# One lane of four looked up whole, three lanes gathered over all partitions, in the edge layer of a graph network

## The chip, the cores and the metric

The kernel runs on one core of one Trainium2 chip. The metric is device time in microseconds (us) for one whole execution, lower is better. All views below come from one profiled execution, whose trace holds start, length and semaphore events of every instruction.

## The reference, cut to what matters

```python
h = maximum(layernorm(x), 0)                                  # 12500 nodes x 32
e = concatenate([h[src], h[dst], edge_attr], axis=-1)         # 400000 edges x 96, dst is sorted
v = relu(e @ W1 + b1) @ W2 + b2                               # 96 -> 64 -> 32
out = x + maximum(segment_max(v, dst), x)                     # per node, the maximum over its edges
```

For every edge, layer one needs the row of `h` of its source node. The sources are random, so these 400000 rows of 32 floats have to be fetched one by one. Everything is f32.

## The kernel before, in words

**Tiling.** The 400000 edges are cut into 4 lanes of 100000 (A = 4), one for each quarter of the 128 partitions (32 features each). A *pair* is two blocks (g = 0 and 1) of 512 edges in each lane, so 4096 edges. There are 96 full pairs (0 to 95), a short one (96) and four mini pairs (97 to 100). In what follows a pair has its number in the program, j.

**Two ways to fetch a source row.** Of each block of 512 edges in each lane, 384 are *gathered* (GATHERED): GpSimd (POOL) issues indirect DMAs of 128 rows each, 12 a block, 24 a pair, one for each of 12 columns of indices (`gather_burst`, the calls at L665), into the ring `src_in` of 7 slots (AHEAD). The gathers of a pair may start once its ring slot has been turned (`src_turned`), and each burst of 2 waits for a count of looked-up tiles (`gather_pair`, L682). VectorE transposes a slot into `src_t` (`turn_src`, L1278). The other 128 edges of each block and lane (4 x 128 = 512 a block) are *looked up*: TensorE multiplies the table of all nodes, held in SBUF, with one-hot columns (`look_up`, L925, matmuls at L939; 98 of them a pair, 128x128 by 512 columns, in four chunks c = 0 to 3). The one-hot columns come from ScalarE (L848, L853) and VectorE (L1251); VectorE then picks from the looked-up rows (`mask_rows`, L1265, at L1269 and L1276) and leaves `picked_rows`, in which all 128 partitions hold a share of a row, so that the matmul with `w_src` (the weights stacked four times) sums over all 128.

**Layer one** of a pair (`layer_one`, L945): for each lane a and block g, W1's three parts are added up in the bank `ps_hid[a]`, half g: edge features (L954, 32 rows x 64 columns of weights, 512 columns of edges), destination (L958, the same), gathered sources (L964, 384 columns), looked-up sources (L969, all 128 rows, 128 columns each, 8 matmuls). The matmuls of 32 rows work side by side in 8 parts of the array (4 lanes x 2 blocks), those of 128 rows in 2 (the blocks). The profile counts each f32 matmul as two. After each lane `hid_summed` lets ScalarE apply the ReLU (`relu_pair`, L834). TensorE's order in pair j is: layer one of j, chunk 0 of the look-up of j+2, layer two of j (L1007), chunks 1 to 3 of the look-up of j+2. Pairs 97 to 100 have no gathered edges (`layer_one_mini`, L981, L983, L987: there all matmuls write half 0, one after the other).

**Loads.** SyncE (SP) issues nearly all loads and stores in one written-out order (`feed`, L591): edges, first rows, picks for j+3, then, for j % 7 == 4 (IX_AT), it waits for the gathers of pair j+2 (the last ring slot) and loads the next 7 pairs' indices (`load_indices`, L450, 4 DMAs at L453), then the mask of j+2 (L477) and the store of j. At k = 1 to 11 of the first turn one more large DMA each fills `run_max` (L622). At the start SP and ScalarE load the first indices (L494, L768, two DMAs each), wait for them, and only then issue the loads of `dst` (L496, L770).

**The end.** When enough pairs are stored, POOL gathers each node's maximum (L749, 98 indirect DMAs, the last 7 only after all 101 pairs are stored), VectorE adds bias and x in 14 steps (L1475 to L1479), and the result is stored.

## Time and profile before

| what | us |
|---|---|
| median of 3 runs | 3179.54 (3175.47 to 3183.26) |
| the profiled execution, its own time | 3179.01 |
| its span in the trace | 3177.2 |
| PE busy (matmuls) | 3042.7 (96%) |
| POOL busy | 2387.1 (75%) |
| DVE (VectorE) busy | 2212.8 (70%) |
| ACT (ScalarE) busy | 2182.5 (69%) |
| mean granted share of TensorE's clock | 0.983 |

How to read it: the busy share of POOL counts only the instructions; the pause after each of them, in which its queue fetches and prepares the next, is not counted. A busy PE is one on which some matmul is under way, and several can be at once. What sets the time has to be read from waits and from the pace of each engine.

### The profile page before, as it was taken

The numbers are of one execution on the slowest core, as the hardware profiler recorded it, in microseconds if no ns is written. First come the engines' busy times: TensorE is split into PE (matmuls) and PEld (weight loads), VectorE is DVE, ScalarE is ACT, GpSimd is POOL, SyncE is SP. The second block draws the span as 40 slices with busy tenths as digits, with TensorE's granted clock in tenths as the row PEclk, the third lists the DMA queues.
The fourth block names the chain that finished last, engine by engine and source line by source line (L and its number), as shares of the span: only waits on it lengthen the run. The fifth ranks groups of instructions, "written<-read, shape, count | busy, mean of one in ns | idle before, by whom it ended". The sixth has DMA issues, their size and how long they took to land.

```text
span 3177.2 us, 59073 instructions
## 1 busy us (share of the span) xinstructions
PE 3042.7 (96%) x19778; PEld 2247.9 (71%) x19778; DVE 2212.8 (70%) x2474; ACT 2182.5 (69%) x2555; POOL 2387.1 (75%) x2523
## 2 busy tenths in 40 slices
PE   6999899998999999999999999999898897999996
PEld 4776677776777777777777777777676675777674
DVE  5321677776777777777777777777675775777666
ACT  3334677776777777777777777777676675777674
POOL 7777677777777777777777777777777777777776
PEclk9999999999999999999999999999999998999998
DMA  8951355444343333334443334333342443333323
GB/s 255 357 201 27 75 138 136 130 117 116 96 104 103 99 96 97 99 102 104 103 104 98 101 101 103 98 96 95 97 103 51 127 102 80 96 103 100 78 65 65
DMA packets 226637, 350.67 MB, mean 110 GB/s; under 512 B 97248, under 2 KB 147708, under 8 KB 226346
## 3 DMA queue, kind: packets, MB, share of 16 engines
q1 hardware_dynamic: 142691, 303.74, 32.6%
q0 software_dynamic: 80448, 41.33, 8.2%
q10 hardware_dynamic: 3332, 4.01, 0.5%
q14 instruction: 139, 1.14, 0.1%
q8 instruction: 27, 0.44, 0.1%
HBM read 240.36 MB, written 119.78 MB: 113 GB/s over the span
## 4 chain that ended last, share of the span: by engine, by line
PE 87%; POOL 5%; DVE 2%; issue 2%; DMA 2%; SPq 1%; ACTq 0%; ACT 0%; POOLq 0%; DVEq 0%
PE ps_rows L939 66%; PE ps_layers L913 4%; PE ps_layers L919 4%; PE ps_layers L954 3%; PE ps_layers L969 3%; PE ps_layers L1007 3%; PE ps_layers L958 3%; POOL src_in L749 3%; POOL src_in L665 2%; PE ps_layers L964 2%; SPq L463 1%; DVE onehot L1251 1%; DMA src_in<-h_dram,src_ix 1%; DMA picks<-picks_dram 0%; DMA dst_i<-in_dst_dram 0%
## 5 line engine op out<-in xcount | busy, mean ns | idle before, releaser
L665 POOL DMA_INDIRECT src_in<-h_dram,src_ix x2269 | 2144.9, 945 | 700.9 <-issue 629.5
L939 PE MATMUL ps_rows<-onehot,table 128*128 128x512 f32 x9898 | 2317.8, 393 | 54.0 <-DVE onehot L1251 54.0
L939 PEld LDWEIGHTS ps_rows<-onehot,table 128*128 128x128 f32 x9898 | 1851.1, 189 | 536.1 <-issue 109.5
L853 ACT ACTIVATE onehot<-distance 128x1024 fp32r<-128x1024 bf16 x909 | 905.4, 1049 | 686.7 <-PE ps_rows L939 681.5
L848 ACT ACTIVATE distance<-picks,below_column 128x1024 bf16<-128x1024 int16 x909 | 983.7, 1136 | 67.8 <-DMA picks<-picks_dram 67.8
L1251 DVE SCALAR_TENSOR_TENSOR onehot<-picks,column,ps_layers 128x1024 fp32r<-128x1024 int16 x404 | 507.6, 1277 | 315.7 <-PE ps_rows L939 302.3
L1301 DVE STREAM_TRANSPOSE ps_layers<-rows_in 128x512 f32<-128x512 f32 x202 | 133.2, 705 | 262.9 <-ACT hid L839 194.4
L1306 DVE TENSOR_TENSOR_SCAN dst_t<-mask_in,dst_t,ps_layers 128x512 f32<-128x512 bf16 (+1 forms) x198 | 250.6, 1266 | 7.3
L839 ACT ACTIVATE hid<-ps_layers,b_col 128x512 f32<-128x512 f32 (+1 forms) x404 | 238.1, 665 | 25.4 <-PE ps_layers L969 13.8
L1319 DVE TENSOR_TENSOR_SCAN max_t<-mask_in,max_t,ps_layers 128x512 f32<-128x512 bf16 x196 | 248.8, 1269 | 4.1 <-PE ps_layers L1007 0.2
L1269 DVE SCALAR_TENSOR_TENSOR picked_rows<-picks,fold,ps_rows 128x512 f32<-128x512 int16 x202 | 141.8, 743 | 113.8 <-PE ps_rows L939 113.8
L1324 DVE STREAM_TRANSPOSE rows_in<-max_t 128x512 f32<-128x512 f32 x202 | 216.8, 1112 | 3.5
L1292 DVE STREAM_TRANSPOSE ea_t<-rows_in 128x512 f32<-128x512 f32 x202 | 204.7, 1086 | 0.0
L825 ACT ACTIVATE signs<-ps_layers,below_node 128x640 bf16<-128x640 f32 x98 | 77.7, 793 | 170.1 <-PE ps_layers L919 162.4
L913 PE MATMUL ps_layers<-ea_t,rows_in 125*128 125x320 bf16 x980 | 153.5, 303 | 25.4 <-DVE rows_in L1076 20.5
L1286 DVE STREAM_TRANSPOSE src_t<-src_in 128x384 f32<-128x384 f32 x193 | 154.4, 871 | 25.4 <-DMA src_in<-h_dram,src_ix 25.4
L919 PE MATMUL ps_layers<-dst_t,rows_in 125*128 125x320 bf16 x980 | 151.2, 302 | 0.0
L1276 DVE COPY_PREDICATED picked_rows<-of_side,ps_rows 128x512 f32<-128x512 int16 x202 | 136.8, 732 | 18.9 <-DVE picked_rows L1269 18.6
L913 PEld LDWEIGHTS ps_layers<-ea_t,rows_in 125*128 125x128 bf16 x980 | 96.2, 99 | 66.2 <-issue 21.1
L954 PE MATMUL ps_layers<-ea_t,w_edge 32*64 32x512 f32 x1552 | 110.7, 627 | 26.4 <-DVE onehot L1251 26.4
L1260 DVE SCALAR_TENSOR_TENSOR of_side<-picks,fold,ps_layers 128x1024 int16<-128x1024 int16 x101 | 128.7, 1274 | 0.0
L1174 DVE TENSOR_SCALAR tmp<-above 128x7 f32<-128x7 f32 x14 | 2.6, 183 | 177.1 <-ACT block L827 177.1
(145 smaller groups left out, 1146.5 us busy)
## 6 DMA issues: line engine op xcount, KB each, us to landing
picks<-picks_dram SPq DMA_DIRECT2D x101, 512.0 KB
first_rows<-hid SPq DMA_DIRECT2D x100, 500.0 KB
rows_in<-in_edge_attr_dram SPq DMA_DIRECT2D x384, 128.0 KB
rows_in<-first_rows SPq DMA_DIRECT2D x384, 128.0 KB
run_max<-rows_in SPq DMA_DIRECT2D x384, 128.0 KB
src_in<-h_dram,src_ix POOLq DMA_INDIRECT x2269
mask_in<-mask_dram SPq DMA_DIRECT2D x384, 64.0 KB
run_max<-in_edge_attr_dram SPq DMA_DIRECT2D x10, 1024.0 KB
```

The source lines that it names most:

```text
L665: pool.indirect_dma_start(out=src_in[:, slot, g, r, :], out_offset=None, in_=rows[:, :], in_offset=bass.IndirectOffsetOnAxis(ap=src_ix[:, ...
L839: nc.scalar.activation(hid[rows, a, columns], ps_hid[a][rows, columns], ACT.Relu, bias=b1_col[rows, 0:1]).then_inc(hid_made, 1)
L848: nc.scalar.activation(distance[:, k, :], picks[:, slot, 0, :, :].rearrange("p g w -> p (g w)"), ACT.Abs, bias=below_column[:, i:i + 1]).t ...
L853: nc.scalar.activation(onehot[:, RING_AT[c] + BY_DVE[c] + k, :, :].rearrange("p g w -> p (g w)"), distance[:, k, :], ACT.Relu, bias=1.0, s ...
L913: nc.tensor.matmul(ps_hid[j % 2 * 2 + half][:, 0:HALF + half], step[:, hb % 2, t, k * P:(k + 1) * P], rise_hi[:, t, half * HALF:(half + 1) ...
L919: mm = nc.tensor.matmul(ps_hid[j % 2 * 2 + half][:, 0:HALF], step[:, hb % 2, t, k * P:(k + 1) * P], rise_lo[:, t, half * HALF:(half + 1) * ...
L939: mm = nc.tensor.matmul(ps_rows[g][side][:, 0:WIDE], table[:, i * SIDES + side, part, :], onehot[:, RING_AT[c] + t, g, :], start=(i + part ...
L954: nc.tensor.matmul(ps_hid[a][g * HID:(g + 1) * HID, :], w_edge[chunk(a), :], ea_t[chunk(a), slot, g, :], start=True, stop=False)
L1251: compared = V.scalar_tensor_tensor(out=onehot[:, RING_AT[c] + t, :, :].rearrange("p g w -> p (g w)"), in0=picks[:, slot, 0, :, :].rearran ...
L1306: V.tensor_tensor_scan(dst_t[:, slot, g, 0:n], mask_in[:, slot, g, 0:n], ps_first[:, g, 0:n], state, ALU.min, ALU.max).then_inc(dst_filled ...
L1319: V.tensor_tensor_scan(max_t[:, g, 0:n], mask_in[:, slot, g, 0:n], v[g][:, 0:n], state, ALU.min, ALU.max).then_inc(max_scanned, 2 // len(c ...
L1324: V.transpose(max_out[:, slot, h, :, :], of_half(max_t[:, :, :], h)).then_inc(max_turned, 1)
```

## The change

The lanes are no longer all treated alike. In a full pair, lanes 0 to 2 have all 512 edges of a block gathered: the first 384 into their own quarter of the partitions as before, the other 128 into the fourth quarter (columns a*4 to a*4+3 of its 12 index columns). Lane 3 (WHOLE) has all 512 looked up. The number of indirect DMAs (24 a pair), of looked-up columns and of one-hot work stays. In layer one the gathered part becomes 6 matmuls of 384 columns (32 rows), each counting up a new semaphore `own_summed`; then 2 matmuls of 128 rows by 512 columns for lane 3; then, after a wait of TensorE on `own_summed`, 6 matmuls of 32 rows by 128 columns that read the rest of lanes 0 to 2 from the fourth quarter of `src_t`, 4 neighbouring columns out of every 12. Lane 3 is now the first for which `hid_summed` counts up, and ScalarE takes the lanes in the order 3, 0, 1, 2. The index loads become 6 DMAs in place of 4 (three of 48-byte pieces, three of 16-byte pieces); the load of the looked-up indices becomes one DMA in place of four. The short and the mini pairs stay as they were.

```diff
--- before.py
+++ after.py
@@ -370,7 +373,9 @@
...
         ea_view, first_view, max_view = (row_view(t) for t in (edge_attr, first_rows, run_max))
-        ix_view = [bass.AP(src.tensor, STARTS[a], [[GATHERS, LANES], [BLK, 2 * SHORT_AT + 1], [1, GATHERS]]).bitcast(U32) for a in range(A)]
+        ix_view = [bass.AP(src.tensor, STARTS[a], [[GATHERS, LANES], [BLK, 2 * SHORT_AT], [1, GATHERS]]).bitcast(U32) for a in range(WHOLE)]
+        rest_ix_view = [bass.AP(src.tensor, STARTS[a] + GATHERED, [[PICKS, LANES], [BLK, 2 * SHORT_AT], [1, PICKS]]).bitcast(U32) for a in range(WHOLE)]
+        half_ix_view = [bass.AP(src.tensor, STARTS[a] + tail_start(SHORT_AT), [[GATHERS, LANES], [1, GATHERS]]).bitcast(U32) for a in range(A)]
         short_ix_view = [bass.AP(src.tensor, STARTS[a] + tail_start(SHORT_AT) + BLK, [[1, LANES], [1, 1]]).bitcast(U32) for a in range(A)]
...
@@ -404,6 +409,14 @@
...
         OUT_STORES = A * len(OUT_BATCHES) + 1
+        def own_ix(a, half):
+            return src_ix[chunk(a), half, :, :, :].rearrange("l s g r -> l (s g) r")
+        def rest_ix(a, half):
+            return src_ix[chunk(WHOLE), half, :, :, a * PICKS:(a + 1) * PICKS].rearrange("l s g r -> l (s g) r")
         def by_rows(t, r):
...
@@ -448,11 +461,13 @@
             def load_indices(j, half, loaded, last=False):
-                blocks = 2 * AHEAD - 3 if last else 2 * AHEAD
-                for a in range(A):
-                    sp.dma_start(src_ix[chunk(a), half, :, :, :].rearrange("l s g r -> l (s g) r")[:, 0:blocks],
-                                 ix_view[a][:, bass.ds(j * 2, blocks)]).then_inc(loaded, D)
-                    if last:
+                blocks = 2 * AHEAD - 4 if last else 2 * AHEAD
+                for a in range(WHOLE):
+                    sp.dma_start(own_ix(a, half)[:, 0:blocks], ix_view[a][:, bass.ds(j * 2, blocks)]).then_inc(loaded, D)
+                    sp.dma_start(rest_ix(a, half)[:, 0:blocks], rest_ix_view[a][:, bass.ds(j * 2, blocks)]).then_inc(loaded, D)
+                if last:
+                    for a in range(A):
+                        sp.dma_start(src_ix[chunk(a), half, AHEAD - 2, 0, :], half_ix_view[a]).then_inc(loaded, D)
                         sp.dma_start(src_ix[chunk(a), half, AHEAD - 2, 1, 0:1], short_ix_view[a], allow_slow_non_contiguous=True).then_inc(loaded, D)
...
@@ -490,19 +505,20 @@
...
                              bass.AP(x.tensor, 0, [[HB * F, LANES - FULL_Q - 1], [1, HB * F]])).then_inc(x_loaded, D)
-            for a in range(A // 2):
-                sp.dma_start(src_ix[chunk(a), 0, 0, :, :], ix_view[a][:, 0:2]).then_inc(first_ix_loaded, D)
-            sp.wait_ge(first_ix_loaded, A * D)
+            for a in range(WHOLE):
+                sp.dma_start(own_ix(a, 0)[:, 0:2], ix_view[a][:, 0:2]).then_inc(first_ix_loaded, D)
+            sp.wait_ge(first_ix_loaded, 2 * WHOLE * D)
             sp.dma_start(dst_i[1:1 + PIECE, 0:SEARCH], dst_before[0:PIECE]).then_inc(dst_loaded, D)
             sp.dma_start(dst_i[1 + PIECE:BP, 0:SEARCH], dst_before[PIECE:BP - 1]).then_inc(dst_loaded, D)
-            for a in range(A):
-                sp.dma_start(src_ix[chunk(a), 0, 1:AHEAD, :, :].rearrange("l s g r -> l (s g) r"), ix_view[a][:, 2:2 * AHEAD]).then_inc(early_ix_loaded, D)
+            for a in range(WHOLE):
+                sp.dma_start(own_ix(a, 0)[:, 2:2 * AHEAD], ix_view[a][:, 2:2 * AHEAD]).then_inc(early_ix_loaded, D)
+                sp.dma_start(rest_ix(a, 0)[:, 2:2 * AHEAD], rest_ix_view[a][:, 2:2 * AHEAD]).then_inc(early_ix_loaded, D)
             sp.wait_ge(dst_loaded, 4 * D)
...
             clear(0, 3)
-            for a in range(A):
-                sp.dma_start(pick_i[0:SHORT_AT, :, a, :], bass.AP(src.tensor, STARTS[a] + GATHERED, [[2 * BLK, SHORT_AT], [BLK, 2], [1, PICKED]])).then_inc(picks_read, D)
+            sp.dma_start(pick_i[0:SHORT_AT, :, :, :].rearrange("j g a e -> j (g a e)"),
+                         bass.AP(src.tensor, STARTS[WHOLE], [[2 * BLK, SHORT_AT], [1, 2 * BLK]])).then_inc(picks_read, D)
             for g, at in enumerate((GATHERED, BLK + SHORT_GATHERED)):
...
@@ -764,9 +780,9 @@
...
         def _(act):
-            for a in range(A // 2, A):
-                act.dma_start(src_ix[chunk(a), 0, 0, :, :], ix_view[a][:, 0:2]).then_inc(first_ix_loaded, D)
-            act.wait_ge(first_ix_loaded, A * D)
+            for a in range(WHOLE):
+                act.dma_start(rest_ix(a, 0)[:, 0:2], rest_ix_view[a][:, 0:2]).then_inc(first_ix_loaded, D)
+            act.wait_ge(first_ix_loaded, 2 * WHOLE * D)
             act.dma_start(dst_i[0:PIECE, SEARCH:SEARCH + BE], dst_rows[0:PIECE]).then_inc(dst_loaded, D)
...
@@ -831,11 +847,12 @@
...
             act.wait_ge(weights_loaded, D * (3 * A + 5))
-            def relu_pair(j, mini=False):
+            def relu_pair(j, mini=False, short=False):
                 wait(act, v_summed, j)
                 rows, columns = (slice(0, HID), slice(0, MINI)) if mini else (slice(0, P), slice(0, BLK))
-                for a in range(A):
-                    act.wait_ge(hid_summed, j * A + (a + 1))
+                order = list(range(A)) if mini or short else [WHOLE, *range(WHOLE)]
+                for n, a in enumerate(order):
+                    act.wait_ge(hid_summed, j * A + (n + 1))
                     nc.scalar.activation(hid[rows, a, columns], ps_hid[a][rows, columns], ACT.Relu, bias=b1_col[rows, 0:1]).then_inc(hid_made, 1)
...
@@ -958,7 +975,28 @@
...
                 pe.wait_ge(src_turned, j * 2 + 2)
-                gathered = [GATHERED, SHORT_GATHERED if short else GATHERED]
+                if short:
+                    short_sources(j, slot)
+                    return
+                for g in range(2):
+                    for a in range(WHOLE):
+                        nc.tensor.matmul(ps_hid[a][g * HID:(g + 1) * HID, 0:GATHERED], w_src[chunk(a), :], src_t[chunk(a), g, :],
+                                         start=False, stop=False).then_inc(own_summed, 1)
+                pe.wait_ge(rows_masked, j * MASKS + MASKS)
+                for g in range(2):
+                    mm = nc.tensor.matmul(ps_hid[WHOLE][g * HID:(g + 1) * HID, :], w_src[:, :], picked_rows[:, slot, g, :], start=False, stop=True)
+                mm.then_inc(hid_summed, 1)
+                pe.wait_ge(own_summed, j * (2 * WHOLE) + 2 * WHOLE)
+                for a in range(WHOLE):
+                    for g in range(2):
+                        rest = src_t[chunk(WHOLE), g, :].rearrange("p (l r) -> p l r", r=GATHERS)[:, :, a * PICKS:(a + 1) * PICKS]
+                        mm = nc.tensor.matmul(ps_hid[a][g * HID:(g + 1) * HID, GATHERED:BLK].rearrange("p (l r) -> p l r", r=PICKS),
+                                              w_src[chunk(WHOLE), :], rest, start=False, stop=True)
+                    mm.then_inc(hid_summed, 1)
+            def short_sources(j, slot):
+                gathered = [GATHERED, SHORT_GATHERED]
                 for g in range(2):
```

## Rows read from the trace of the kernel before

**Rows 1.** The page: busy time, the chain that ended last, the ReLUs' group.
```profile
PE 3042.7 (96%) x19778; PEld 2247.9 (71%) x19778; DVE 2212.8 (70%) x2474; ACT 2182.5 (69%) x2555; POOL 2387.1 (75%) x2523
PE 87%; POOL 5%; DVE 2%; issue 2%; DMA 2%; SPq 1%; ACTq 0%; ACT 0%; POOLq 0%; DVEq 0%
...
L839 ACT ACTIVATE hid<-ps_layers,b_col 128x512 f32<-128x512 f32 (+1 forms) x404 | 238.1, 665 | 25.4 <-PE ps_layers L969 13.8
```

**Rows 2.** Timeline, PE: layer one's first matmuls (start, length) of pairs 14, 68, 69, 76, 83, 95, 96.
```profile
761.04 0.69 PE L954 MATMUL ps_layers<-ea_t,w_edge 32*64 32x512 f32 x8
2233.79 0.68 PE L954 MATMUL ps_layers<-ea_t,w_edge 32*64 32x512 f32 x8
2272.67 0.68 PE L954 MATMUL ps_layers<-ea_t,w_edge 32*64 32x512 f32 x8
2483.21 0.69 PE L954 MATMUL ps_layers<-ea_t,w_edge 32*64 32x512 f32 x8
2694.87 0.69 PE L954 MATMUL ps_layers<-ea_t,w_edge 32*64 32x512 f32 x8
3034.41 0.69 PE L954 MATMUL ps_layers<-ea_t,w_edge 32*64 32x512 f32 x8 [1.42 <-DVE onehot L1251]
3061.69 0.69 PE L954 MATMUL ps_layers<-ea_t,w_edge 32*64 32x512 f32 x8
```

**Rows 3.** POOL: busy time and count in one stretch; all gathers of L665 by form.
```profile
500.00:2900.00 2400.00, 1814.20 (x1923) 0.99 0.40 101
L665 POOL DMA_INDIRECT src_in<-h_dram,src_ix x2269: 938/944/1618, 72.7 to 3043.3; - x190
L665 POOL DMA_INDIRECT src_in<-in_x_dram,src_ix x48: 940/944/2412, 3.3 to 66.4; - x48
```

**Rows 4.** Waits from 290 us on: of PE; of DVE from 470 to 3045 us; of SP's queue.
```profile
PE ps_rows L939 <- DVE onehot L1251: 54.0, 5, 17.8
PE ps_layers L954 <- DVE onehot L1251: 26.4, 7, 9.0
...
DVE ps_layers L1301 <- DMA mask_in<-mask_dram: 68.4, 3, 26.0
DVE src_t L1286 <- DMA src_in<-h_dram,src_ix: 25.4, 6, 5.7
...
SPq L608 <- DMA src_in<-h_dram,src_ix: 160.3, 9, 32.9
```

**Rows 5.** Timeline, PE, of layer one in an undisturbed pair (j = 42) and after it.
```profile
1524.69 1.11 PE L954 MATMUL ps_layers<-ea_t,w_edge 32*64 32x512 f32 x16
1525.60 1.06 PE L958 MATMUL ps_layers<-dst_t,w_dst 32*64 32x512 f32 x16
1526.46 0.85 PE L964 MATMUL ps_layers<-src_t,w_src 32*64 32x384 f32 x16
1527.24 1.09 PE L969 MATMUL ps_layers<-picked_rows,w_src 128*64 128x128 f32 x16
1528.26 3.92 PE L939 MATMUL ps_rows<-onehot,table 128*128 128x512 f32 x16
```

**Rows 6.** Timeline, PE, of the looked-up matmuls of a mini pair (one column half only).
```profile
3089.96 1.96 PE L987 MATMUL ps_layers<-picked_rows,w_src 128*64 128x128 f32 x16
3091.85 0.50 PE L939 MATMUL ps_rows<-onehot,table 128*128 128x512 f32 x1
```

**Rows 7.** Timeline of the start (0 to 16 us), and of SP around its one long block.
```profile
0.76 0.87 SPq L494 DMA_DIRECT2D src_ix<-in_src_dram  x2
3.08 0.37 ACTq L770 DMA_DIRECT2D dst_i<-in_dst_dram  x1
...
671.64 1.90 SPq L453 DMA_DIRECT2D src_ix<-in_src_dram  x4
...
688.16 23.69 SPq L463 DMA_DIRECT2D rows_in<-in_edge_attr_dram  x4
...
731.88 2.02 PE L954 MATMUL ps_layers<-ea_t,w_edge 32*64 32x512 f32 x16 [8.99 <-DVE onehot L1251]
```

**Rows 8.** Timeline of the end: last stores, start of VectorE's last steps, POOL, last step.
```profile
3148.62 5.42 SPq L586 DMA_DIRECT2D run_max<-rows_in  x8
3152.49 0.19 DVE L1466 COPY ps_rows<-b_row 128x32 f32<-128x32 f32 x1
3155.91 0.26 SPq L642 DMA_DIRECT2D carry<-run_max  x1
3158.19 1.16 POOL L749 DMA_INDIRECT src_in<-run_max,gather_ix  x1 [0.30 <-issue]
3168.35 0.39 DVE L1475 TENSOR_TENSOR src_in<-src_in,ps_rows 128x224 f32<-128x224 f32 x1 [0.65 <-DMA src_in<-run_max,gather_ix]
```

More of the change, by code:

```diff
@@ L37 @@
 PICKED = PICKS * LANES
+WHOLE = A - 1
+assert A * PICKED == BLK and WHOLE * PICKS == GATHERS
 MINIS = 4
@@ L350, in build @@
         hid_summed, hid_made, v_summed, layers_begun = sem("hid_summed"), sem("hid_made"), sem("v_summed"), sem("layers_begun")
+        own_summed = sem("own_summed")
         max_scanned, max_turned, ends_set = sem("max_scanned"), sem("max_turned"), sem("ends_set")
@@ L692, in gather_turn @@
             def gather_turn(turn, half, loads, last=False):
-                pool.wait_ge(ix_loaded[half], loads * (A * D))
+                pool.wait_ge(ix_loaded[half], loads * (2 * WHOLE * D) + last * (2 * A * D))
                 pool.sem_inc(gathers_begun, 1)
@@ L698, in gather_turn @@
                     gather_pair(half, slot, turn * (AHEAD * TILES) + (slot + 2 - AHEAD) * TILES - SLACK, last and slot == AHEAD - 2)
-            pool.wait_ge(first_ix_loaded, A * D)
+            pool.wait_ge(first_ix_loaded, 2 * WHOLE * D)
             gather_early(0)
-            pool.wait_ge(early_ix_loaded, A * D)
+            pool.wait_ge(early_ix_loaded, 2 * WHOLE * D)
             for j in range(1, RAW_PAIRS):
@@ L735, in _ @@
                 gather_turn(i * 2 + 2, 0, i + 1)
-            gather_turn(TURNS - 1, 1, TURNS // 2 + 1, last=True)
+            gather_turn(TURNS - 1, 1, TURNS // 2, last=True)
             pool.wait_ge(low_row_written, D)
@@ L854, in one_hot, with pair @@
                                          distance[:, k, :], ACT.Relu, bias=1.0, scale=-1.0).then_inc(act_onehot_made, 1)
-            def pair(j, slot, turn, next_again=True, after_next=True, mini=False):
-                relu_pair(j, mini)
+            def pair(j, slot, turn, next_again=True, after_next=True, mini=False, short=False):
+                relu_pair(j, mini, short)
                 if next_again:
@@ L881, in _ @@
             for j in range(SHORT_AT, PAIRS):
-                pair(j, j % 2, j // 2, next_again=j + 2 < PAIRS, after_next=j + 3 < PAIRS, mini=j > SHORT_AT)
+                pair(j, j % 2, j // 2, next_again=j + 2 < PAIRS, after_next=j + 3 < PAIRS, mini=j > SHORT_AT, short=j == SHORT_AT)
             act.wait_ge(onehot_made, PAIRS * DVE_ALL)
@@ L1126, in _ @@
             V.memset(table_f[:, UNITS - 1, :], 0.0).then_inc(table_padded, 1)
-            dve.wait_ge(picks_read, (A + 3) * D)
+            dve.wait_ge(picks_read, 4 * D)
             V.tensor_copy(pick_16[:, :], pick_i[:, :, :, :].rearrange("j g a e -> j (g a e)")).then_inc(pick_step, 1)
```

## The prediction

> **What bounds the kernel now.** I read the page first. TensorE is busy 96% of the span and fills 87% of the chain that ended last, POOL 5% [rows 1]. That reads as "TensorE is the bound", and it is half the truth, so I took the pace of each engine next. TensorE: from pair 14 to pair 68 are 54 pairs in 2233.79 - 761.04 = 1472.75 us, 27.27 us a pair [rows 2]. POOL: 1923 gathers in 2400 us, 1.248 us each although one is busy for only 0.944 [rows 3], and with 24 gathers 29.95 us a pair. POOL is the slower of the two by 2.68 us a pair; its 75% is a full engine. It is hidden at first because the gathers have a head start of up to seven ring slots.
>
> How far ahead POOL is can be worked out. Its last gather is number 2269 + 48 = 2317, starts at 3043.3 [rows 3], and pair j's last gather is number 24(j + 1), so it ends at 3043.3 - (2317 - 24(j + 1)) x 1.248 + 0.9. For pair 68 that is 2219.3, and TensorE begins its layer one at 2233.79 [rows 2]: a lead of 14.5 us. For pair 95 it is 3028.0, against 3034.41: 6.4 us, which is what landing, transposes and the one-hot columns behind them take. So the lead is used up towards the end and TensorE waits. Its waits are always booked on VectorE's one-hot (L1251), 54.0 and 26.4 us [rows 4]; but VectorE itself was held by mask loads (68.4 us in 3 waits) and by gathers (25.4 us in 6). The mask loads are late because SP, before every seventh pair's index load, sits until the gathers of two pairs ahead have landed (L608, up to 32.9 us), with that mask queued behind. Once the lead falls under about 24 us, this blocks: pair 69 starts at 2272.67 where 2261.06 was due, with a lead of 23.4; the blocks before pairs 76 and 83 leave 24 to 26.3 [rows 2]. Together: 81 pairs from pair 14 at 27.27 would bring pair 95 to 2970.2; it starts at 3034.41. **64.2 us of TensorE's time are slack behind the gathers.** That is the number on which the change turns.
>
> At the end three ends nearly meet: the last store and with it the signal for POOL's last 7 gathers falls at about 3155.9, POOL gets to them at 3158.19, and VectorE's last steps, begun at 3152.49, wait 0.65 us for the last gather [rows 8]. If TensorE is late by X, the end is late by X - 0.65.
>
> **The change, term by term.** First layer one of a full pair [rows 5].
>
> (1) *Gathered part*, 6 matmuls instead of 8: no gain. The 8 run side by side; edges and destination take 0.86 to 0.91 us for two turns (high and low part) of 512 columns, so 0.43 a turn, and 384 columns 0.32. With the fourth quarter idle a turn is as long.
>
> (2) *Looked-up part.* Now 8 turns of 128 columns (each with both halves side by side), 1.02 us from first start to the next look-up. In a mini pair the 16 have only one half, one after another: 1.89 us [rows 6]. The difference, 0.87 us for 8 turns, gives 0.109 us a turn, and 1.02 - 8 x 0.109 = 0.15 us for coming into and out of such a phase. After the change: 2 turns of 512 columns, 0.86 in place of 0.87: -0.01.
>
> (3) *The rest*, 6 matmuls of 128 columns in the fourth quarter. They share it, so both halves run side by side but the three lanes and the two parts one after another: 6 turns x 0.109 = 0.65 us, plus 0.15 for one more phase. Nothing hides it: the matmuls before and after use all rows. +0.80. The reads jump by 12 columns after every 4, which no matmul here does. From below such a turn costs 0.109, as the contiguous 128 columns of [rows 5, 6]; from above I bound it by a matmul over the whole 384 columns that the read steps across, 0.32 us a turn, +1.28 more a pair. I take the lower end, as the nearest row in columns moved. By the Trainium skill (page "SBUF — State Buffer", the note on SBUF cachelines) the SBUF is read in 16-byte lines and four f32 may be strided over for free, which here would be the lower end too, as each run of four begins on such a line; no row here shows it.
>
> (4) *The new wait* on `own_summed`: behind it on TensorE are the rest, the look-up, everything. But it asks for matmuls that ended before the looked-up phase (0.86 us) began: 0.
>
> (5) *Order of the ReLUs*: ScalarE gets lane 3 first and lanes 0 to 2 within the next 0.65 us; its four ReLUs (0.665 us each [rows 1], 2.7 in all) are needed only by layer two, behind 32 look-up matmuls (16 take 3.9 us [rows 5]). 0. With that cover gone, the later start would cost its 0.65 us.
>
> So TensorE needs **0.79 us more a pair**, for 96 pairs.
>
> (6) *Start.* SP and ScalarE issue three index DMAs each instead of two before the loads of dst; two take 0.87 us [rows 7], so +0.43 before everything. The picks' load, one DMA for four, lies behind cover: no row has anything waiting for it.
>
> (7) *Index loads in the loop*: 4 DMAs take 1.90 us, 6 take 2.85, every seventh pair. The index DMAs stand ahead of the mask load and the store; the mask of pair j+2 is needed only about a pair later, so 0.95 us is covered except in the three blocks, where it would be added each time; these vanish, see below. 0. POOL's gathers stay 24 a pair of 128 rows: 0.
>
> (8) *SP's long issue* at 688.16 (23.69 us) behind the last large fill stops TensorE once for 8.99 us [rows 7]. It stays, but is hung on pair 11's store, and TensorE is one pair's 0.79 later when it gets there: -0.8.
>
> **The sum.** Before pair 95's layer one lie 95 x 0.79 = 75.0; less 0.8, plus 0.43, less the slack of 64.2: +10.4. Pair 95 itself +0.79, the last slack -0.65: **+10.6 us**. Against the profiled execution's 3179.01 (0.5 under the median of 3179.54): 3189.6; I say 3190 for the median.
>
> Check that the slack is really free: the blocks go, as with +0.79 a pair the lead at pair 83 would be -26 (761.04 + 69 x 27.27 = 2642.9 against 2668.6) + 66 - 1 = 39 us, above 26. At pair 95 it is 16, above 6.4: TensorE is then the bound, by 9 us. POOL's own end moves by +0.43 and, since early gathers wait for a transposed ring slot, by about one pair's 0.79.
>
> **The rivals.** All turn on the extra time d of a pair. TensorE's end moves by 96 d - 65.2; the gathers' end by about +1.4; they meet at d = 0.69, and 0.3% (9.5 us, about what a measurement can tell from no change) is reached at d = 0.78.
>
> *A. Forecast*, d 0.72 to 0.87: +4 to +18, centre +10.6. Chance 0.50.
>
> *B. Not slower: the gathers still set the end.* Place: the last pairs and POOL's tail; price +1.4 us, so about 3181; it decides for d under 0.69, for instance if the switch out of the looked-up phase is partly covered (its 0.15 off gives d = 0.64), or if SP's one long block no longer reaches TensorE (-9 us, from 10.6 to 1.6). For it: the 64.2 us are real and the margin small. Against: the 0.65 us of turns alone are nearly 0.69, and a third phase has never been free in these rows. 0.22.
>
> *C. The six counts of `own_summed` hold up the switch.* They fall within one turn, right before the looked-up phase, where now none falls. Price between 0, as the phase start already waits a little for VectorE, and one more phase change of 0.15 a pair: 96 x 0.15 = +14, so +25, 3204. For: no row has six counts together; against: counts of single matmuls cost nothing visible in [rows 5]. 0.17. The Trainium skill (page "TensorE: Matmul & The Clock Gate", section "The cost: per-tile semaphore tail") says that such increments are written one after another, 26.3 ns each; by an estimate from that page six would add 0.16 us a pair, and the sum would be about +26.
>
> *D. The jumping reads are slow*: up to 1.28 a pair more, +134 us; even a quarter of it +41. 0.08.
>
> *E. Faster* by over 9.5 us: would need POOL's pace to change, and nothing touches it. 0.03.
>
> **How the numbers follow.** Prediction 3190, A's centre. Slower by over 0.3%: a bit over half of A (0.28), C, D: 0.53. Within 0.3%: rest of A, B: 0.44. Faster 0.03. The range 3180 to 3210 leaves out D, E and C's upper part. A alone: 3184 to 3198.
>
> **What would show it.** Right: pairs 28.06 us apart; L939 following three phases instead of two; the rest 0.80 us; the three late blocks gone, PE's waits down from 80 to under 35 us; PE not waiting before pair 95, a lead there of about 16 us; POOL waiting before its last 7 gathers. B: pairs under 27.96 apart and pair 95 still about 6 us behind its gathers. C: the gap between gathered and looked-up phase longer than the 0.78 us of now. D: the rest's turns longer than 0.109. Wrong altogether if POOL's 1.248 us moves.

## The result, and the profile after

The changed kernel takes 3187.88 us (median of 8 runs, 3185.26 to 3189.22) against 3179.04 (8 runs, 3175.47 to 3183.26) for the kernel before: a ratio of 1.0027, interval 1.0016 to 1.0037, or 8.8 us slower. That interval straddles the 0.3% below which I had said a measurement could not tell it from no change, but it does not reach 1: the change makes the kernel a little slower. One execution of all, of the run with the rest in its own quarter below, took 4330.07 us at a granted clock of 0.667, and is left out of its median. The profiled execution took 3185.75 us with a span of 3183.9; that of before 3179.01 with 3177.2, so the two traces differ by 6.7 us. Everything below is read from these two traces unless it says otherwise.

From the page of the changed kernel: the busy row, the shares of the chain that ended last, and the groups of the look-up's and layer one's first matmuls (columns: busy us, mean ns | idle us before them, and what ended it).

```profile
PE 3104.8 (98%) x19394; PEld 2237.0 (70%) x19394; DVE 2210.6 (69%) x2474; ACT 2181.9 (69%) x2555; POOL 2392.4 (75%) x2523
PE 95%; DVE 2%; DMA 1%; SPq 1%; issue 0%; ACTq 0%; ACT 0%; DVEq 0%
...
L956 PE MATMUL ps_rows<-onehot,table 128*128 128x512 f32 x9898 | 2308.5, 392 | 10.1 <-DVE onehot L1289 10.1
...
L971 PE MATMUL ps_layers<-ea_t,w_edge 32*64 32x512 f32 x1552 | 109.8, 622 | 15.9 <-DVE onehot L1289 15.9
```

Beside [rows 1] and [rows 4]: TensorE is busy for 62.1 us more with 384 matmuls fewer, its waits on the one-hot columns went from 80.4 to 26.0 us, and POOL, 5% of the chain before, is in it no longer. (The profile writes each f32 matmul down twice, so these are 384 records.) TensorE paid for the change mainly with time in which it had been waiting. The 54.4 us of waits that went are not all of the 64.2 us of slack, though. The other 10 were lost in the kernel before when TensorE came back from a wait at half its clock. In its timeline the stop before pair 69 reads

```profile
2261.18 11.56 PE L939 MATMUL ps_rows<-onehot,table 128*128 128x512 f32 x42 [9.56 <-DVE onehot L1251]
```

9.56 us of waiting, and pair 69 came 11.61 us late. The granted clock was 0.50 (1.2 GHz) from 2255 to 2264 us, in the wait and for 2.8 us of work behind it, 0.78 up to 2266, and 1.00 (2.4 GHz) from there to 2273. Over the whole span the granted clock is 0.991 in the changed kernel, for 0.983.

The price of a pair comes first, from the timeline of TensorE: pairs 14, 68, 95 and 96 (start, length), which answer to [rows 2].

```profile
769.40 0.69 PE L971 MATMUL ps_layers<-ea_t,w_edge 32*64 32x512 f32 x8
...
2283.92 0.68 PE L971 MATMUL ps_layers<-ea_t,w_edge 32*64 32x512 f32 x8
...
3041.18 0.69 PE L971 MATMUL ps_layers<-ea_t,w_edge 32*64 32x512 f32 x8
...
3069.22 0.69 PE L971 MATMUL ps_layers<-ea_t,w_edge 32*64 32x512 f32 x8
```

The 54 pairs take 1514.52 us, 28.047 each; before it was 27.273. So d = 0.774 us, and it stays so to the end: pair 95 begins 28.04 before pair 96, where [rows 2] had lost 64.2 us on the way. (d is the extra time of a pair, as in the prediction.) Where the 0.774 lie is in TensorE's timeline of one undisturbed pair, which answers to [rows 5].

```profile
1526.66 1.11 PE L971 MATMUL ps_layers<-ea_t,w_edge 32*64 32x512 f32 x16
1527.57 1.06 PE L975 MATMUL ps_layers<-dst_t,w_dst 32*64 32x512 f32 x16
1528.43 0.84 PE L983 MATMUL ps_layers<-src_t,w_src 32*64 32x384 f32 x12
1529.20 1.08 PE L987 MATMUL ps_layers<-picked_rows,w_src 128*64 128x512 f32 x4
1530.21 0.87 PE L993 MATMUL ps_layers<-src_t,w_src 32*64 32x128 f32 x12
1531.01 3.24 PE L956 MATMUL ps_rows<-onehot,table 128*128 128x512 f32 x13
```

From start to start: gathered 0.77 (before 0.78), looked-up 1.01 (1.02), and the new phase, the rest, 0.80. The two old phases kept their lengths to the hundredth, though one has a quarter of its matmuls fewer and the other went from 16 to 4 records; the third came on top whole.

What stood behind the gathers before now stands in front of them. These are waits of TensorE and of SP's queue from 290 us on, and of VectorE from 470 to 3052 us (in total, times, longest), beside [rows 4].

```profile
PE ps_layers L971 <- DVE onehot L1289: 15.9, 2, 8.9
PE ps_rows L956 <- DVE onehot L1289: 10.1, 2, 5.1
...
SPq L624 <- DMA src_in<-h_dram,src_ix: 28.0, 3, 15.0
...
DVE ps_layers L1339 <- ACT hid L856: 195.1, 92, 5.4
```

SP's wait for gathers fell from 160.3 us in 9 to 28.0 in 3, and VectorE's 68.4 us on mask loads and 25.4 on gathers have no row any more. TensorE's remaining 26.0 us are waits at the start and the one behind SP's long block. The end, beside [rows 8], from the timeline of VectorE and of POOL:

```profile
3160.04 0.17 DVE L1504 COPY ps_rows<-b_row 128x32 f32<-128x32 f32 x1
...
3164.18 0.95 POOL L765 DMA_INDIRECT src_in<-run_max,gather_ix  x1 [2.60 <-SPq L657]
```

POOL, which came to its last 7 gathers late in [rows 8], now stands there for 2.60 us waiting for SP's signal: it is ahead.

### The profile page after: what moved, and what is told of

Its sections match the earlier page's. It is cut to its first block, busy times and chain, and to the rows that moved or that the text cites. A ratio compares the mean times of both kernels' runs of the same rounds, so it can differ in the third digit from the quotient of the medians.

```text
span 3183.9 us, 58462 instructions
## 1 busy us (share of the span) xinstructions
PE 3104.8 (98%) x19394; PEld 2237.0 (70%) x19394; DVE 2210.6 (69%) x2474; ACT 2181.9 (69%) x2555; POOL 2392.4 (75%) x2523
## 4 chain that ended last, share of the span: by engine, by line
PE 95%; DVE 2%; DMA 1%; SPq 1%; issue 0%; ACTq 0%; ACT 0%; DVEq 0%
PE ps_rows L956 71%; PE ps_layers L930 4%; PE ps_layers L936 4%; PE ps_layers L971 3%; PE ps_layers L1045 3%; PE ps_layers L987 3%; PE ps_layers L975 3%; PE ps_layers L993 2%; PE ps_layers L983 2%; SPq L478 1%; DMA picks<-picks_dram 0%; DMA dst_i<-in_dst_dram 0%; DVE onehot L1289 0%; DMA x_again<-in_x_dram 0%; ACTq L833 0%
```

## The experiments

Each run was compared with the kernel before on its own chip, whose median differs between chips (3177.72, 3183.19 and 3184.25 for the runs below): ratios are to be compared, and the traces' own times more than either.

### Two gathers fewer a pair: is POOL the bound of before and not of after?

The twelfth gather of each block is not issued, so a pair has 22. The rows that it would have brought count as zero: a part of the gathered sources is left out of layer one. On the kernel before:

```diff
+ISSUED = GATHERS - 1
...
             def gather_row(half, slot, g, r, rows=h_dram):
+                if r == GATHERS - 1:
+                    return
...
-                        dve.wait_ge(src_gathered[k % AHEAD][g], turn * (2 * D * GATHERS) + (k // AHEAD + 1) * (D * GATHERS))
+                        dve.wait_ge(src_gathered[k % AHEAD][g], turn * (2 * D * ISSUED) + (k // AHEAD + 1) * (D * ISSUED))
```

> The kernel before with 22 gathers a pair instead of 24 (the twelfth index column of each block isn't fetched, its rows stay zero). My theory (the gather stream is what TensorE waits for, 64 us of slack): POOL needs 22 x 1.248 = 27.5 us a pair, about TensorE's 27.27, so the lead is never used up, the three late blocks and the waits before pairs 91 to 95 go, and the time falls by about 60 us, to 3110 to 3125. Rival (TensorE is the bound as the page's 96% suggests, and its late waits come from SP's order and not from the gathers' pace): within 5 us of before.

Measured: 3112.74 us against 3183.19, ratio 0.9776 (0.976 to 0.9792), 70.5 us faster. From this run's timeline and waits of TensorE:

```profile
760.31 0.68 PE L960 MATMUL ps_layers<-ea_t,w_edge 32*64 32x512 f32 x8
...
2969.44 0.69 PE L960 MATMUL ps_layers<-ea_t,w_edge 32*64 32x512 f32 x8
...
PE ps_layers L960 <- DVE onehot L1258: 16.7, 2, 9.7
PE ps_rows L945 <- DVE onehot L1258: 10.0, 2, 5.1
```

The 81 pairs from 14 to 95 take 2209.13 us, 27.273 each, with no late stop among them; pair 95 begins at 2969.44, where the prediction had worked out 2970.2 for a TensorE that waits for no gather. TensorE's waits are 26.7 us, those of the changed kernel. The 64.2 us are slack behind the gathers, and this run shows it from the side of POOL. The spans of the two traces differ by 65.6 us (3111.6 for 3177.2); the medians differ by more because the kernel before takes 3183.19 on this chip.

The same edit on the changed kernel, with the same rows left out:

> The changed kernel with the same 22 gathers a pair. My theory (with 28.05 us a pair TensorE alone sets the end): no more than 3 us faster than the changed kernel, so 3183 to 3189, and about 70 us (96 x 0.77, less what the gathers' start gives) slower than the same edit on the kernel before. Rival (the gathers still set part of the time after the change): 10 us or more faster than the changed kernel.

Measured: 3187.78 us, ratio 1.0014 (1.0004 to 1.0023), pairs 28.047 us apart, pair 95 at 3043.39: the changed kernel's time, with two gathers fewer. It is 75.0 us behind the run above; 96 pairs at 0.774 are 74.3. So the change costs TensorE all of its 0.774 us a pair, and the kernel as a whole shows only the few us that stand out over the slack.

### What in the third phase costs the 0.80 us

First, the rest in its own lanes' quarters: each lane's 128 last columns are taken from its own gathered rows, of which they read the first 128 a second time, and its six matmuls follow the gathered part at once. Layer one's sum of the last 128 columns of three lanes so holds other rows; the number and the size of the matmuls are the same. Two more things change with the order: TensorE no longer waits on `own_summed`, and ScalarE starts its four ReLUs, in the order 0 to 3, only behind the looked-up matmuls.

```diff
+                for g in range(2):
+                    for a in range(WHOLE):
+                        mm = nc.tensor.matmul(ps_hid[a][g * HID:(g + 1) * HID, GATHERED:BLK], w_src[chunk(a), :], src_t[chunk(a), g, 0:PICKED],
+                                              start=False, stop=True)
+                mm.then_inc(hid_summed, 1)
                 pe.wait_ge(rows_masked, j * MASKS + MASKS)
...
-                pe.wait_ge(own_summed, j * (2 * WHOLE) + 2 * WHOLE)
```

> The changed kernel, but the 6 matmuls of 128 columns for the rest of lanes 0 to 2 read (other) data from their own lanes' quarters, right behind the 384 columns and ahead of the looked-up phase: the same number of matmuls and columns, but side by side in six parts of the array and with no phase change of their own, so what is computed for these edges is wrong. My theory (the 0.77 us a pair are the six turns one after another in one quarter, 0.65, and one more phase change, 0.15): the pair's extra falls to two turns, about 0.2 us (period 27.45 to 27.55), the gathers set the end again, and the time is that of before plus 0 to 3 us, 3178 to 3183. Rival (the cost is the new order, the semaphore own_summed with its six counts, or lane 3's late sum): the pair stays above 27.9 us, 3184 or more.

Measured: 3183.51 us against 3183.19, ratio 1.0001 (0.9992 to 1.0011), pairs 27.467 us apart. The time lies 0.5 us over the range that I had expected, and close to the rival's, because the kernel before is slow on this chip; the 27.467, which the rival had over 27.9, is what decides. TensorE's timeline of a pair:

```profile
1535.31 0.84 PE L983 MATMUL ps_layers<-src_t,w_src 32*64 32x384 f32 x12
1535.96 0.42 PE L987 MATMUL ps_layers<-src_t,w_src 32*64 32x128 f32 x12
1536.30 1.08 PE L992 MATMUL ps_layers<-picked_rows,w_src 128*64 128x512 f32 x4
```

Side by side and in the gathered phase, the same six matmuls cost 0.19 us instead of 0.774. With only that on TensorE the gathers set the end again: the late stops are back (16.9 us before pair 76, 21.9 before 83), pair 95 begins 6.2 us behind its gathers, for 6.4 before, and the time is that of before.

Next, the same reads, but in a phase of their own behind the looked-up matmuls, so that only the quarter differs from the changed kernel. Again the last 128 columns of three lanes take other rows:

```diff
-                        rest = src_t[chunk(WHOLE), g, :].rearrange("p (l r) -> p l r", r=GATHERS)[:, :, a * PICKS:(a + 1) * PICKS]
+                        rest = src_t[chunk(a), g, 0:PICKED].rearrange("p (l r) -> p l r", r=PICKS)
...
-                                              w_src[chunk(WHOLE), :], rest, start=False, stop=True)
+                                              w_src[chunk(a), :], rest, start=False, stop=True)
```

> The changed kernel, order and waits untouched, but each rest matmul reads (other) data from its own lane's quarter with that quarter's weights, so that the six work side by side though still in a phase of their own behind the looked-up one. Together with the run that also moved them ahead (pair 27.47 us) it splits the 0.77 us: theory, the turns one after another in one quarter are 6 x 0.109 and shrink to 2 x 0.109 = 0.22, the phase change of 0.15 stays, so a pair is 27.27 - 0.01 + 0.22 + 0.15 = 27.63 us, and as that is below 27.96 the gathers set the end: time of before within 3 us. Rival (a phase of its own costs more, and the turns less): 27.75 us or more.

Measured: 3183.33 us against 3184.25, ratio 1.0001 (0.9991 to 1.0011), pairs 27.680 us apart. TensorE's timeline of a pair:

```profile
1544.26 1.08 PE L987 MATMUL ps_layers<-picked_rows,w_src 128*64 128x512 f32 x4
1545.27 0.46 PE L993 MATMUL ps_layers<-src_t,w_src 32*64 32x128 f32 x12
1545.66 6.68 PE L956 MATMUL ps_rows<-onehot,table 128*128 128x512 f32 x28
```

The phase takes 0.39 us from start to start instead of 0.80. The pair lies between my 27.63 and the rival's 27.75. The two runs split d: 0.37 us for turns taken one after another in one quarter (28.047 - 27.680), 0.21 for a phase of its own behind matmuls of 128 rows (27.680 - 27.467), 0.19 for the turns that there would be in any place (27.467 - 27.273). Only the first is a difference in one thing. The wait on `own_summed` and the order of the ReLUs change together with the place, so that the 0.21 is put down to the phase change because no wait of TensorE shows at that place in the traces, and not because a run changed it alone. By turns of 0.109 the first would be 4 x 0.109 = 0.44, the last 2 x 0.109 = 0.22; they came out a little cheaper, and the phase change dearer than my 0.15. The Trainium skill (page "TensorEngine Tiling (Array Packing)", section "Key Properties") says that changing the tiling mode drains TensorE; the 0.21 us is what one more such phase, with the change into it and out of it, was worth here, and the traces agree that it is not free.

Then the jumping reads, rival D. The rest reads 128 neighbouring columns of the fourth quarter, so again other rows enter the last 128 columns of three lanes:

```diff
-                        rest = src_t[chunk(WHOLE), g, :].rearrange("p (l r) -> p l r", r=GATHERS)[:, :, a * PICKS:(a + 1) * PICKS]
+                        rest = src_t[chunk(WHOLE), g, a * PICKED:(a + 1) * PICKED].rearrange("p (l r) -> p l r", r=PICKS)
```

> The changed kernel whose rest matmuls read 128 neighbouring columns of the fourth quarter instead of 4 out of every 12 (so the rows that lanes 0 to 2 get for these edges are not theirs). Theory (jumps of 12 columns after every 4 are free): pairs 28.05 us apart, time of the changed kernel within 3 us. Rival D in small (the jump costs something within the 0.80 us): the rest's phase shorter than 0.80 us.

Measured: 3187.72 us, ratio 1.0032 (1.002 to 1.0044), pairs 28.047 us apart, and in TensorE's timeline the rest again takes 0.80 us:

```profile
1532.44 0.87 PE L993 MATMUL ps_layers<-src_t,w_src 32*64 32x128 f32 x12
1533.24 3.01 PE L956 MATMUL ps_rows<-onehot,table 128*128 128x512 f32 x12
```

Runs of four f32 with steps of twelve cost nothing here. This is what the note on cachelines of the Trainium skill (page "SBUF — State Buffer") would give for runs that begin on a line of 16 bytes; no run tried shorter runs. D is out.

### The wait and its counts

Rival C said that six counts just ahead of the looked-up phase hold up the switch. One count on the last gathered matmul in their place:

```diff
-                        nc.tensor.matmul(ps_hid[a][g * HID:(g + 1) * HID, 0:GATHERED], w_src[chunk(a), :], src_t[chunk(a), g, :],
-                                         start=False, stop=False).then_inc(own_summed, 1)
+                        own = nc.tensor.matmul(ps_hid[a][g * HID:(g + 1) * HID, 0:GATHERED], w_src[chunk(a), :], src_t[chunk(a), g, :],
+                                               start=False, stop=False)
+                own.then_inc(own_summed, 1)
...
-                pe.wait_ge(own_summed, j * (2 * WHOLE) + 2 * WHOLE)
+                pe.wait_ge(own_summed, j + 1)
```

> The changed kernel with one count of own_summed, on the last of the six gathered matmuls, instead of six. In the changed kernel the looked-up phase starts 0.77 us after the gathered one, as before (0.78), so the six counts should cost nothing: pairs stay 28.05 us apart, the time that of the changed kernel (3185 to 3190). Rival C of the prediction (six counts hold up the switch): up to 0.15 us a pair less, and up to 14 us faster.

Measured: 3188.01 us, ratio 1.0032 (1.002 to 1.0045), pairs 28.047 us apart, every phase as long as in the changed kernel:

```profile
1530.38 0.84 PE L983 MATMUL ps_layers<-src_t,w_src 32*64 32x384 f32 x12
1531.16 1.08 PE L988 MATMUL ps_layers<-picked_rows,w_src 128*64 128x512 f32 x4
1532.17 0.87 PE L994 MATMUL ps_layers<-src_t,w_src 32*64 32x128 f32 x12
```

C is out. The section "The cost: per-tile semaphore tail" of the Trainium skill (page "TensorE: Matmul & The Clock Gate"), read as a cost of this place, gave an estimate of 0.16 us a pair for six counts; the runs show nothing of it, with six or with one (28.047 us a pair in both).

That left the order. With the rest directly behind the gathered part, two phases of 32 rows stand together, which I expected to save one phase change; the price would be a wait that is no longer covered by the looked-up matmuls.

```diff
                                          start=False, stop=False).then_inc(own_summed, 1)
-                pe.wait_ge(rows_masked, j * MASKS + MASKS)
...
                 pe.wait_ge(own_summed, j * (2 * WHOLE) + 2 * WHOLE)
...
                     mm.then_inc(hid_summed, 1)
+                pe.wait_ge(rows_masked, j * MASKS + MASKS)
```

> The changed kernel with the rest's 6 matmuls right behind the gathered ones, in the same 32-row phase, and the looked-up 2 matmuls last; ReLUs in the order 0, 1, 2, 3. One phase change fewer (0.15 us a pair), but now the wait on own_summed stands directly behind the matmuls that count it, so their way through the array (a 384-column matmul is booked 0.48 us where its turn takes 0.32) lies open, about 0.16 plus the count. Theory: the two about cancel, a pair is 27.95 to 28.1 us, the time within 5 us of the changed kernel. Rival 1 (only the phase change counts): 27.9 us a pair, 14 us less for TensorE, of which the gathers leave about 7: 3178 to 3183. Rival 2 (the looked-up rows' wait for VectorE was on the way, and is now covered too): a further 0.05 a pair less.

Measured: 3215.03 us against 3177.72, ratio 1.0121 (1.0105 to 1.0136), pairs 28.354 us apart: 0.31 us more than the changed kernel, where I had expected about none. TensorE's timeline of a pair and, below, the row of its waits:

```profile
1512.74 0.84 PE L983 MATMUL ps_layers<-src_t,w_src 32*64 32x384 f32 x12
1513.81 0.87 PE L989 MATMUL ps_layers<-src_t,w_src 32*64 32x128 f32 x12 [0.23 <-PE ps_layers L983]
1514.61 1.08 PE L994 MATMUL ps_layers<-picked_rows,w_src 128*64 128x512 f32 x4
1515.62 7.55 PE L956 MATMUL ps_rows<-onehot,table 128*128 128x512 f32 x32
...
PE ps_layers L989 <- PE ps_layers L983: 22.2, 96, 0.2
```

The rest starts 1.07 us after the gathered part, of which two turns of 384 columns are 0.64. That leaves 0.43 us, in the place of the 0.13 that the step to the looked-up phase took in the changed kernel (0.77 - 0.64), and so the pair is 0.30 us longer. Of the 0.43 the wait's row shows 0.23 a pair. That the other 0.20 belong to the wait as well, as the end of the last matmul and the start of the next, is my reading: no run has this order without the wait, and the nearest, the rest in its own quarter, had 0.65 us from start to start with none. The rest itself still takes 0.80 and the looked-up part 1.01. So term (4) of the prediction, the wait at 0, holds only because looked-up matmuls stand between; this run is that cover taken away.

### The start, and an attempt at POOL's one hold

The changed kernel began pair 0 2.34 us earlier than before, and the load of the looked-up indices (the picks) is the only part of the start that the change makes smaller. Four loads of 512-byte pieces again:

```diff
-            sp.dma_start(pick_i[0:SHORT_AT, :, :, :].rearrange("j g a e -> j (g a e)"),
-                         bass.AP(src.tensor, STARTS[WHOLE], [[2 * BLK, SHORT_AT], [1, 2 * BLK]])).then_inc(picks_read, D)
+            for a in range(A):
+                sp.dma_start(pick_i[0:SHORT_AT, :, a, :], bass.AP(src.tensor, STARTS[WHOLE] + a * PICKED, [[2 * BLK, SHORT_AT], [BLK, 2], [1, PICKED]])).then_inc(picks_read, D)
```

> The changed kernel with the looked-up indices loaded by four DMAs of 512-byte pieces, as before, instead of one of 4096-byte pieces. In the trace of the changed kernel the reload of the table from h_dram starts 3.2 us earlier than before (67.2 against 70.5 us) and layer one of pair 0 at 363.8 instead of 366.1, though the loads of dst start 0.5 us later. Theory (the one large DMA clears the queues sooner for the store of h): both go back, the table's reload to about 70.5, pair 0 to about 366.5, and the time is 2 to 3 us longer than the changed kernel's. Rival (scatter from run to run): no shift of more than 1 us in the median, and pair 0 starts anywhere from 363 to 367.

Measured: 3188.0 us, ratio 1.0015 (1.0005 to 1.0024); pair 0 begins at 365.03. The two kernels were then run again, with a profile each, to see how far two executions of one kernel differ:

> The changed kernel once more, for the scatter of its start and of the gathers' pace. Theory: pairs 28.05 us apart as always, the start of pair 0 anywhere from 363 to 367 us, the median within 1 us of 3188 whatever the chip. Rival: the pace of the pairs itself scatters.

> The kernel before once more, with its trace. Theory: pairs 27.27 us apart up to pair 68, then waits; pair 0 starts anywhere from 363 to 367 us (no gain of the changed kernel's start), and its median differs from chip to chip by a few us (3179 and 3183 so far) because it ends with the gathers. Rival: pair 0 again at 366 and the table's reload at 70.4 us, so that the changed kernel's earlier start is real.

Measured: 3187.25 us, ratio 1.0013 (1.0004 to 1.0023), for the changed kernel, and 3183.22, ratio 1.0 (0.999 to 1.0009), for the one before. Pair 0 began at 365.57 in the changed kernel and at 363.94 in the one before, the other way round than in the first two traces; over all thirteen traces it lies between 363.8 and 366.6 with no order by kernel. No shift of 2.34 us between the kernels is left over this scatter, and nothing speaks for the theory of the picks' load any more.

Last, an attempt to win something at POOL, whose gathers are held once at 350 us for 7.5 us. The hold seemed to be the count of look-up tiles, so the kernel before was run with gathers released 13 tiles earlier:

```diff
-SLACK = 6
+SLACK = 19
```

> The kernel before with SLACK 19 instead of 6: each burst of gathers is released 13 looked-up tiles (one pair) earlier; the ring slot's own wait for the transposes stays. Theory (the gather stream sets the end of the kernel before, and the only time it stands still is about 9 us between 300 and 480 us, held by TensorE's tile count): the standstill shrinks by up to 9 us and the time with it, 3170 to 3180 against about 3179 to 3183. Rival (the hold is the ring slot, not the tile count, or TensorE and not the gathers sets the end): no change beyond 2 us.

Measured: 3177.53 us against 3177.72, ratio 1.0001 (0.9992 to 1.001). POOL came to this gather 4.7 us earlier, and its hold is 3.5 us longer. From POOL's timeline of this run:

```profile
357.77 0.95 POOL L665 DMA_INDIRECT src_in<-h_dram,src_ix  x1 [10.98 <-PE ps_rows L939]
```

in the kernel before, the same gather stood as

```profile
358.99 0.94 POOL L665 DMA_INDIRECT src_in<-h_dram,src_ix  x1 [7.47 <-PE ps_rows L939]
```

The release waits on something that the tile count does not move, and the traces point at the ring slot. In both traces 168 gathers stand before this one, 7 slots of 24, so it is the first that needs a slot a second time. VectorE begins the two transposes of `src_t` at 356.43 us in the kernel before and at 355.23 in this run, and the gather starts 2.56 and 2.54 us behind that. The slot was not released earlier in a run of its own. No version that computes the whole and beats the kernel before was found.

## Why the prediction was right

**What it turned on held.** The hinge was stated as 96 d - 65.2 for TensorE's end, with the gathers' end taking over below d = 0.69. The first result and the seven runs made from the changed kernel with all 24 gathers give four values of d, each with the kernel before of its own chip:

```text
kernel                    d       96 d - 65.2   measured against before
rest in own quarter       0.19        -47          +0.3   gathers set the end
own quarter, last         0.41        -26          -0.9   gathers set the end
changed (first result)    0.774        +9.1        +8.8
changed, again            0.774        +9.1        +3.0
changed, four pick loads  0.774        +9.1        +4.8
changed, read straight    0.774        +9.1       +10.0
changed, one count        0.774        +9.1       +10.3
rest ahead of looked-up   1.08        +38.5       +37.3
```

Below the hinge the time doesn't move. Above it, between two kernels on one chip (one count and rest ahead), it grows by 27.0 us for 0.307 us of d, so 88 us per us for the 96 forecast. The five rows at 0.774 spread by 7 us though the five medians of the changed kernel and its variants agree within 1: it is the kernel before that differs from chip to chip. That the first result came so near to the forecast of 10.6 is in part luck, as on another chip the difference was 3.0. Rival B is out for the changed kernel: its pairs are 28.047 apart and pair 95 begins 9.7 us behind its gathers, not 6. Its place was real, though: the runs with the rest in its own quarter are in it.

**Terms (1) to (3), the price of a pair.** Predicted 0.79, measured 0.774. Gathered and looked-up part -0.01 each for the 0 and -0.01 forecast, the rest 0.80 for 0.80. The sum inside the 0.80 was less exact than it looks: the phase change is 0.21 rather than 0.15 (with the reservation above), the turns 0.56 for six rather than 0.65; the two errors have opposite signs.

**Terms (4), (5) and (7)**, at nothing: the timeline agrees, with no stretch beyond the three phases in 28.047 us. Of (4) the cover was named and has now its price, up to 0.43 us a pair. Its reason was stated too strongly: by the run with the rest ahead, the awaited matmuls are not done when the looked-up phase begins. With no cover the rest could start 1.07 us after the gathered part, and the looked-up phase starts 0.77 after it, so some 0.30 of its 1.01 us are used up by it.

**Term (6), the start, was mis-sized.** The loads of dst begin 0.50 us later, for 0.43 forecast, in the timeline of SP:

```profile
3.58 0.33 SPq L511 DMA_DIRECT2D dst_i<-in_dst_dram  x1
```

(In the kernel before SP's first such load stood at 3.08, as ScalarE's in [rows 7].) But pair 0 began 2.34 us earlier, since the start scatters by up to 2.8 us from execution to execution, and a term of 0.4 is lost in it: it is neither borne out nor refuted by pair 0.

**Term (8), SP's long block, was wrong.** I took off 0.8 us because TensorE would come later to a block that stays. TensorE still waits 8.88 us there, for 8.99. The step that failed is the block moving one pair's d less than TensorE: it begins at 695.00 for 688.16, 6.84 us later, and pair 12 begins 6.83 us later too (pair 13 stands 36.99 us behind it for 36.33, at 739.37 for 731.88); the block itself takes 24.09 us for 23.69. From the timeline of SP and of TensorE:

```profile
695.00 24.09 SPq L478 DMA_DIRECT2D rows_in<-in_edge_attr_dram  x4
...
739.37 2.01 PE L971 MATMUL ps_layers<-ea_t,w_edge 32*64 32x512 f32 x16 [8.88 <-DVE onehot L1289]
```

The time lost there (the period of pair 12 over the usual one) is 8.2 to 9.8 us over all thirteen traces, so the 0.1 is scatter too.

**The sum of the profiled executions.** Pair 95 begins 6.77 us later than before, where +10.4 was forecast: -1.5 for 95 times (0.774 - 0.79), -2.8 for the start, +0.7 for the block make 6.8. The last pair adds 0.77, the 0.65 us of waiting in [rows 8] are gone, which makes 6.9, and the end comes 6.7 us later. The medians are 8.8 apart, closer to the 10.6 forecast, because this execution of the changed kernel lies 2.1 us under its own median.

**What I said the trace would show.** Pairs at 28.06, three phases, the rest 0.80, the three late blocks gone, waits under 35 us (26.0), POOL waiting before its last 7 gathers: all there. The lead at pair 95 was to be 16 us and is 9.7. TensorE's part of the miss is 3.6 us, the same three differences as in the sum above; POOL's is the rest, as its last gather for pair 95 ends at 3031.5 and not, as the prediction's working gives with its +1.2, at 3029.2. All gathers of the main loop by form, beside [rows 3]:

```profile
L681 POOL DMA_INDIRECT src_in<-h_dram,src_ix x2269: 943/947/1587, 69.5 to 3046.8; - x190
```

The median is 947 ns for 944, and the last gather starts at 3046.8 for 3043.3. The step "POOL's own end moves by +0.43" and a pair's 0.79 gave 1.2; it moved 3.5, and the difference is no more than the gathers' pace varies by itself, as the last section shows.

## What to carry to other kernels

When an engine is busy for 96% and another for 75%, compare their paces per unit of work before naming the bound, and work out how much of the busy engine's time is slack behind the other; a change on the busy engine is then free up to slack divided by passes (here 64.2 / 96, 0.67 us a pair) and costs its full price beyond. Small matmuls that leave part of the rows empty are cheap where they can run side by side inside a phase of their own shape, and cost several times that (0.19 against 0.77 us a pair) in one quarter and a phase apart. Before moving such a phase, look at what it hides: a wait of TensorE for matmuls that it has just issued cost nothing behind 0.86 us of other work, and between 0.23 and 0.43 without.

## What the runs showed that was not expected

**The gathers have two paces.** In the traces one takes 944 or 947 ns (as the median of 2269), and with the pause between them 1.2487 or 1.2511 us. Both kernels show both: the kernel before in its first trace and in its repetition above (947 for 944), the changed kernel at 947 in both of its traces and at 944 where only the rest's reads were straightened. Over some 2320 gathers that is 5.6 us. From the repetition of the kernel before:

```profile
L665 POOL DMA_INDIRECT src_in<-h_dram,src_ix x2269: 943/947/1667, 68.9 to 3046.0; - x190
...
3037.55 0.69 PE L954 MATMUL ps_layers<-ea_t,w_edge 32*64 32x512 f32 x8
```

Its pair 0 began 2.17 us earlier than in the first trace of before, and its pair 95 came 3.14 us later. A kernel that ends with its gathers passes this on, and one that TensorE ends does not: the medians of the kernel before lie between 3177.7 and 3184.3 over the chips used, those of the changed kernel and of its variants with the same 28.047 us between 3187.3 and 3188.0. The ratio is therefore 1.0013 on one chip and, by the run with one count, 1.0032 on another. That the gathers' pace is what makes the chips differ was not shown: the kernel before has only two traces in all, and on two chips both paces occurred among its variants and those of the changed kernel. What sets the pace stays open; no run here was made for it.

**A turn of 32 rows is cheaper than the one that the prediction took.** Two turns of 128 columns added 0.19 us in the gathered phase, and one after another in one quarter they came to some 0.09 each (0.37 for four). The 0.109 of [rows 5, 6] was read from matmuls of 128 rows. Why they differ was not tried.
